# Graph and expert layer on one core: expert rows weighted on the way and added to the output by accumulating scatters, the combining stage removed

## What is computed

```
x1     = x + gnn(layernorm(x)) + attention(layernorm(x))
n      = layernorm(x1);  u = n * gamma + beta
logits = u @ Wr + br;    (top, sec), (e1, e2) = top_k(logits, 2)
w1, w2 = softmax(top, sec)
out    = x1 + w1 * expert[e1](u) + w2 * expert[e2](u)
expert[e](u) = gelu(u @ W1[e] + b1[e]) @ W2[e] + b2[e]
```

## Time and profile before

| | us |
|---|---|
| median of 3 runs | 1534.99 (1532.45 to 1539.14) |
| the profiled execution | 1534.88 |
| its span in the trace | 1532.9 |
| router block's last part, W2 load issued | 985.88 |
| first expert gather issued | 1058.74 |
| last expert scatter issued | 1461.52 |
| first load of the combining block issued | 1473.52 |

### The profile page before, as it was taken

The page is one execution under the profiler, slowest core; times in us unless marked ns, Lnnn a source line. Parts: engine busy times, 40 slices in busy tenths (PEclk is TensorE's granted clock), DMA queues, the critical chain, the costliest instruction groups (busy, mean ns, idle before and its releaser), DMA issues. The chain is left out here.

```text
span 1532.9 us, 30179 instructions
## 1 busy us (share of the span) xinstructions
PE 1266.2 (83%) x8310; PEld 1107.0 (72%) x8311; DVE 960.1 (63%) x2700; ACT 450.8 (29%) x1322; POOL 764.0 (50%) x822
## 2 busy tenths in 40 slices
PE   1797678888888999998987978767999999999910
PEld 1685477887787889887775856523999999999900
DVE  3998777777688888778854977863222223222347
ACT  1565600122123333333221023463322332233200
POOL 2001577777777777777774023201555555555400
PEclk9999898999999999999998989955999999999965
DMA  6002533333466667778895000252666666666658
GB/s 204 15 0 69 168 106 105 104 105 106 126 177 174 199 196 215 211 219 261 279 283 166 1 1 1 108 181 94 211 210 209 216 209 210 212 215 207 192 198 314
DMA packets 142678, 248.24 MB, mean 162 GB/s; under 512 B 22826, under 2 KB 99108, under 8 KB 142324
## 3 DMA queue, kind: packets, MB, share of 16 engines
q1 hardware_dynamic: 99256, 146.13, 29.8%
q0 software_dynamic: 34320, 93.76, 21.0%
q10 hardware_dynamic: 9004, 7.21, 1.4%
HBM read 213.65 MB, written 33.36 MB: 161 GB/s over the span
## 5 line engine op out<-in xcount | busy, mean ns | idle before, releaser
L716 POOL DMA_INDIRECT RG<-table,srci x504 | 496.0, 984 | 157.7 <-issue 154.4
L733 PE MATMUL ps<-S_t,RG 128*128 128x96 f32 x2016 | 283.7, 278 | 51.7 <-DMA RG<-table,srci 47.8
L733 PEld LDWEIGHTS ps<-S_t,RG 128*128 128x128 f32 x2016 | 270.3, 195 | 74.8 <-DMA RG<-table,srci 60.8
L1881 DVE TENSOR_TENSOR R<-ps,R 128x256 f32<-128x256 f32 x105 | 44.6, 425 | 278.4 <-PE ps L1833 278.4
L1823 PE MATMUL ps<-R,RG 128*128 128x128 f32 x1680 | 207.2, 277 | 0.0
L987 DVE TENSOR_TENSOR R<-R,ps 128x392 f32 x280 | 157.0, 561 | 79.3 <-PE ps L743 59.7
L755 PE MATMUL ps<-zrow,R 128*128 128x256 f32 x686 | 193.3, 386 | 12.8 <-DMA zrow<-table 7.9
L1856 ACT ACTIVATE R<-ps,RG 128x128 f32<-128x128 f32 x420 | 119.7, 368 | 279.0 <-PE ps L1823 279.0
L1833 PE MATMUL ps<-R 128*128 x840 | 198.6, 380 | 0.0
L1823 PEld LDWEIGHTS ps<-R,RG 128*128 128x128 f32 x1680 | 198.4, 194 | 0.0
L1907 POOL DMA_INDIRECT results<-R,S_t x105 | 103.7, 988 | 164.0 <-DVE R L1881 160.8
(11 more groups left out here) (352 smaller groups left out, 1883.3 us busy)
## 6 DMA issues: line engine op xcount, KB each, us to landing
RG<-in_w SPq DMA_DIRECT2D x106, 514.0 KB
zrow<-table SPq DMA_DIRECT2D x336, 128.0 KB
R<-results SPq DMA_DIRECT2D x48, 256.0 KB, 12.2
RG<-table,srci POOLq DMA_INDIRECT x504, 3.4
table<-RG SPq DMA_DIRECT2D x12, 512.0 KB, 2.9
table<-R SPq DMA_DIRECT2D x12, 512.0 KB, 3.3
out<-R ACTq DMA_DIRECT2D x48, 128.0 KB, 5.4
R<-in_x SPq DMA_DIRECT2D x6, 896.0 KB
```

The costliest lines, as they stand in the source:

```text
L716: nc.gpsimd.indirect_dma_start(out=grows[:, s, :], out_offset=None, in_=table, in_offset=bass.IndirectOffsetOnAxis(ap=srci[:, ND + q, c:c ...
L733: last = nc.tensor.matmul(window(q % 2)[:, h, :], grows[:, s, h * P:(h + 1) * P], S_t[:, q % 2, c, :], start=c == 0, stop=c == GC - 1)
```

## The change

The DRAM tensor `results` and the combining block are gone. In their place:

- SP stores x1 into the output in the router block, four tiles at a time, as `finish` produces them (`store_x1`). Twelve of the thirteen stores stand ahead of the W2 load on SP's queue.
- `table` becomes `ntable`, with rows of 258 floats: the normalised row and the row's two weights. The weights are stored with two more transfers that write runs of two floats (8 bytes), 6250 in all, between the ninth and the tenth `keep_rows`. VectorE computes the weights behind its second placing round (`row_weights`), for which ScalarE's exponential moves ahead of `norm(24)`.
- In the expert block VectorE picks the weight of the slot (`wsel`, two one-column instructions in `widen`), and behind the bias multiplies the tile by it (`weighted`). `rows` now waits for the bias alone (`b_ok`), the scatter for the product (`y_ok`).
- The scatter adds to the output (`compute_op=ALU.add`). Padding slots get a row number out of bounds, which is skipped. A row's two experts lie in different tiles, and nothing orders two additions to one row but waits, so scatter(t) waits until scatter(t-2) has landed, until `border(t)` on SP has passed (which waits for scatter(t-5), and where a new expert begins for scatter(t-1)), and for the first five tiles for scatter(t-1).
- Of VectorE's steps behind `psI`, the four that made `sct` go. Two new ones for `sct` and three for the selecting columns `first` and `second` stand at the head of VectorE's expert block, and two small ones for the borders ahead of the wait for `psI`.

```diff
-    results = nc.dram_tensor("results", (2 * N + NTILE * P, D), f32, kind="Internal").ap()
+    ntable = nc.dram_tensor("ntable", (N, D + 2), f32, kind="Internal").ap()
...
+                def store_x1(h):
+                    lo, hi = 4 * h, min(4 * h + 4, T)
+                    sp.wait_ge(x_ok, hi)
+                    if hi < T:
+                        sp.dma_start(a_out[lo * P:hi * P, :].rearrange("(t p) f -> p t f", p=P),
+                                     o_all[:, lo:hi, :]).then_inc(x1_out, 16)
+                    else:
+                        sp.dma_start(a_out[lo * P:N, :], o_all[0:TAIL, lo, :]).then_inc(x1_out, 16)
+
+                for h in range(NB4 - 1):
+                    store_x1(h)
                 sp.wait_ge(px_ok, T)
                 sp.dma_start(R3[:, 0:room], a_w2).then_inc(w2_in, 16)
-                sp.wait_ge(x_ok, T)
+                store_x1(NB4 - 1)
                 sp.dma_start(b2s.rearrange("p e f -> p (e f)"), a_b2.unsqueeze(0).to_broadcast([P, NX * D])).then_inc(b2_in, 16)
...
                     if lo + n < T:
-                        sp.dma_start(table[lo * P:(lo + n) * P, :].rearrange("(t p) f -> p t f", p=P),
+                        sp.dma_start(ntable[lo * P:(lo + n) * P, 0:D].rearrange("(t p) f -> p t f", p=P),
                                      n_rows[:, 4 * (h % NR):4 * (h % NR) + n, :]).then_inc(keep[h % NR], 16)
                     else:
-                        sp.dma_start(table[lo * P:N, :], n_rows[0:TAIL, 4 * (h % NR), :]).then_inc(keep[h % NR], 16)
+                        sp.dma_start(ntable[lo * P:N, 0:D], n_rows[0:TAIL, 4 * (h % NR), :]).then_inc(keep[h % NR], 16)
...
                 for h in range(NB4 - 4):
                     keep_rows(h)
+                sp.wait_ge(w_ok, 1)
+                sp.dma_start(ntable[0:(T - 1) * P, D:D + 2].rearrange("(t p) k -> p t k", p=P),
+                             wpair[:, 0:T - 1, :]).then_inc(w_out, 16)
+                sp.dma_start(ntable[(T - 1) * P:N, D:D + 2], wpair[0:TAIL, T - 1, :]).then_inc(w_out, 16)
                 sp.wait_ge(eid_ok, 1)
...
-                for t in range(early):
+                for t in range(24):
                     norm(t)
                 act.wait_ge(ex_in, 1)
                 act.activation(w2c[:, :], sec, ACT.Exp).then_inc(ex_ok, 1)
+                for t in range(24, early):
+                    norm(t)
                 act.wait_ge(ready, 3)
...
+                def row_weights():
+                    v.wait_ge(ex_ok, 1)
+                    ch.done(nc.vector.tensor_scalar(w1c[:, :], w2c[:, :], 1.0, None, ALU.add))
+                    ch.done(nc.vector.reciprocal(wpair[:, :, 0], w1c[:, :]))
+                    ch.done(nc.vector.tensor_tensor(wpair[:, :, 1], w2c[:, :], wpair[:, :, 0], ALU.mult))
+                    v.sem_inc(w_ok, 1)
...
+                def border_waits():
+                    turn = slot[0:1, 0, 0:NTILE]
+                    ch.done(nc.vector.tensor_tensor(turn, eidf[:, 1:NTILE + 1], eidf[:, 0:NTILE], ALU.is_gt))
+                    ch.done(nc.vector.scalar_tensor_tensor(late, turn, 16.0, late_f[:, 0:NTILE], ALU.mult, ALU.add))
+
                 for r in range(NROUND):
                     place(r)
...
+                    if r == WROUND:
+                        row_weights()
+                    if r == EROUND:
+                        expert_ids()
+                border_waits()
...
-                nc.vector.tensor_scalar(pad, held, 0.5, None, ALU.is_lt)
                 ch.done(nc.vector.tensor_scalar(held_i, held, -1.0, 0.0, ALU.add, ALU.max))
                 ch.done(nc.vector.tensor_scalar(gat, held_i, 1, None, ALU.arith_shift_right))
-                ch.done(nc.vector.tensor_tensor(pad, pad, dump, ALU.mult))
-                ch.done(nc.vector.scalar_tensor_tensor(pad, held, -1.0, pad, ALU.add, ALU.add))
-                ch.done(nc.vector.tensor_copy(sct, pad))
...
+                def border(t, s):
+
+                    n = nc.sync.value_load(late[0:1, bass.ds(t - 1, 1)], min_val=16, max_val=16 * (LOOPS + 1))
+                    sp.wait_ge(y_out[s], n)
+                    sp.sem_inc(turn_ok, 1)
+
+                for t in range(2, 9):
+                    fetch(t, t % 4)
+                with nc.sync.Fori(0, LOOPS - 2) as i:
                     for u in range(4):
-                        fetch(i * 4 + (u + 2), (u + 2) % 4)
+                        fetch(i * 4 + (u + 9), (u + 1) % 4)
+                        border(i * 4 + (u + 5), u % 4)
+                for t in range(NTILE - 4, NTILE):
+                    border(t, (t - 1) % 4)
...
-                v.sem_inc(y_ok, 2)
+                ch = Chain(v, dv)
+                ch.done(nc.vector.tensor_scalar(pad, held, 0.5, float(1 << 16), ALU.is_lt, ALU.mult))
+                ch.done(nc.vector.tensor_tensor(sct, pad, gat, ALU.add))
+                ch.done(nc.vector.tensor_scalar(held_i, held_i, 1, None, ALU.bitwise_and))
+                ch.done(nc.vector.tensor_copy(second[:, 0:NTILE], held_i))
...
                 def widen(t, s):
                     v.wait_ge(xt_ps, t + 1)
+                    nc.vector.tensor_scalar(wpart[:, s:s + 1], xr[:, s, D:D + 1], first[:, bass.ds(t, 1)], None,
+                                            ALU.mult).then_inc(wp_ok, 1)
                     for k in range(KC):
-                        last = nc.vector.tensor_scalar(ur[:, s % 2, k, :], psX[s % 2][:, k * P:(k + 1) * P],
-                                                       gamma[:, k:k + 1], beta[:, k:k + 1], ALU.mult, ALU.add)
-                    last.then_inc(u_ok, 1)
-
-                def bias(t, s, turn):
+                        nc.vector.tensor_scalar(ur[:, s % 2, k, :], psX[s % 2][:, k * P:(k + 1) * P],
+                                                gamma[:, k:k + 1], beta[:, k:k + 1], ALU.mult, ALU.add)
+                    v.wait_ge(wp_ok, t + 1)
+                    nc.vector.scalar_tensor_tensor(wsel[:, s:s + 1], xr[:, s, D + 1:D + 2], second[:, bass.ds(t, 1)],
+                                                   wpart[:, s:s + 1], ALU.mult, ALU.add).then_inc(u_ok, 1)
+
+                def weighted(t, s, turn):
                     e = nc.vector.value_load(eid_i[0:1, bass.ds(t, 1)], min_val=0, max_val=NX - 1)
                     v.wait_ge(y_ps, t + 3)
                     if not (isinstance(turn, int) and turn == 0):
                         v.wait_ge(y_out[s], turn * 16)
                     nc.vector.tensor_tensor(yr[:, s, :], psY[s % 2][:, 0:D],
                                             b2s[:, bass.ds(e, 1), :].rearrange("p a f -> p (a f)"),
-                                            ALU.add).then_inc(y_ok, 1)
+                                            ALU.add).then_inc(b_ok, 1)
+                    v.wait_ge(b_ok, t + 3)
+                    nc.vector.tensor_scalar(yr[:, s, :], yr[:, s, :], wsel[:, s:s + 1], None, ALU.mult).then_inc(y_ok, 1)
...
-                        out=xr[:, t % 4, :], out_offset=None, in_=table,
+                        out=xr[:, t % 4, :], out_offset=None, in_=ntable,
                         in_offset=bass.IndirectOffsetOnAxis(ap=gat[:, t:t + 1], axis=0)).then_inc(x_in[t % 4], 16)
 
                 def scatter(t):
-                    pool.wait_ge(y_ok, t + 3)
+                    pool.wait_ge(y_ok, t + 1)
+                    if t >= 2:
+                        pool.wait_ge(y_out[(t - 2) % 4], 16 * ((t - 2) // 4 + 1))
+                    if 1 <= t < 5:
+                        pool.wait_ge(y_out[t - 1], 16)
+                    if t >= 5:
+                        pool.wait_ge(turn_ok, t - 4)
                     nc.gpsimd.indirect_dma_start(
-                        out=results, out_offset=bass.IndirectOffsetOnAxis(ap=sct[:, t:t + 1], axis=0),
-                        in_=yr[:, t % 4, :], in_offset=None).then_inc(y_out[t % 4], 16)
+                        out=a_out, out_offset=bass.IndirectOffsetOnAxis(ap=sct[:, t:t + 1], axis=0),
+                        in_=yr[:, t % 4, :], in_offset=None, bounds_check=N - 1, oob_is_err=False,
+                        compute_op=ALU.add).then_inc(y_out[t % 4], 16)
...
-                def load(t, s, n=P):
-                    sp.dma_start(pairs[0:n, s, :], results[bass.ds(t * (2 * P), 2 * n), :]
-                                 .rearrange("(p k) f -> p (k f)", k=2)).then_inc(got[s], 16)
...
-                def combine(t, s, turn, n=P):
-                    v.wait_ge(got[s], turn * 16 + 16)
-                    x1 = o_all[0:n, bass.ds(t, 1), :].rearrange("p a f -> p (a f)")
-                    nc.vector.scalar_tensor_tensor(slotb[0:n, s % 2, :], pairs[0:n, s, 0:D], w1c[0:n, bass.ds(t, 1)],
-                                                   x1, ALU.mult, ALU.add).then_inc(mid, 1)
-                    v.wait_ge(mid, t + 1)
-                    nc.vector.scalar_tensor_tensor(pairs[0:n, s, 0:D], pairs[0:n, s, D:2 * D],
```

(50 more changed lines are left out.)

55 lines of the change are left out of this document (11 added, 44 removed).

## The result

The changed kernel takes 1524.8 us (median of 6, 1519.14 to 1526.61) against 1534.88 before: a ratio of 0.9929, 95% interval 0.9913 to 0.9945. It is faster by 0.7%, clear of noise, where 4% were forecast. Its profiled execution took 1519.14 us, the fastest of its six, with a span of 1517.2.

What follows compares the result with a forecast made beforehand. TensorE was taken to bound the expert block, ScalarE's wait for a `table` store the router block's end. Less 71.4 us of end, +4.2 for W2, -0.8 behind `psI`, plus the last scatter's needs: 1474 us; range 1468 to 1480, 8 in 10 1467 to 1495.

Steps and rivals of the forecast that it cites:

- The end: Behind the last scatter: all 71.4 us go; the new last scatter is issued at 1465.5, lands 1471.0, span 1472.4.
- W2 behind x1's stores: Router block, SP's queue: W2 and the first row store go later, ScalarE and placing matmuls too; +4.2 us (0 to 6).
- Weights, small writes: Router block: row weights and 6250 writes of 8 bytes (3.4 to 18.7 us) are covered by 35 us; cost nothing.
- Rival B: Small writes outlast the router block, with cover gone at 90 ns each; 1480 to 1500 us, chance 0.13.
- Landing of an addition: Expert block: an adding scatter lands in 4.5 us, bounds 2.7 to 6.1; its wait bites only past 7.1 us.
- Expert block, VectorE: Per tile, product, two one-column steps and waits add 1.0 to 1.4 us against 2.46 of slack; nothing in the period.
- The step that failed: Expert block: a gather delayed behind a border's waiting scatter is made good in the next tile; cost nothing.
- the treatment of POOL: Expert block: POOL idles 1.47 us ahead of each scatter, so its instruction may grow that much from 0.99; cost nothing.
- C: Expert block: the scatter's landing bites a little, or POOL's instruction grows past 2.4 us; 1480 to 1527 us, chance 0.10.
- D: Expert block: chain of scatters waiting for scatter t-2 sets the period, slower than before; landing past 8.3 us, chance 0.06.

Runs made afterwards that it cites:

- its own experiment: Changed kernel with the W2 load issued ahead of the last two stores of x1: 1522.62 us, 0.9925 of the kernel before.
- the shorter delay: Kernel before with one POOL sum of 128x320 (about 0.9 us) between each scatter and the gather behind it: ratio 1.0072.
- the one that copies: Changed kernel with the scatter copying instead of adding, all waits kept: 1488.67 us, 0.9697 of the kernel before.
- the kernel with the delay and the gather ahead: Kernel before with one POOL sum of 128x320 behind each scatter and gather t+5 put ahead of scatter t: ratio 1.0004.

## Why the prediction was wrong

- **The end: mostly right, by two errors of opposite sign.** 60.1 us fell away between last bias and end; forecast were 72.1 less about 8.2. The last scatter started at 1507.05 and landed 2.7 us later, at 1509.75, and the span ended at 1517.2. The prediction had allowed 1.0 + 4.5 us up to the landing, counting POOL's instruction twice, since a landing in these views holds it already, and 1.4 us behind it (1.9, if 1528.6 + 2.4 is the last store's landing); 7.5 us follow instead. They are nearly all one instruction of POOL's own queue at the end of the block, DRAIN; what it waits for the trace doesn't tell. It stood in the trace of before as well, inside the 12.0 us of "clearing and meeting". Its rows by line, after and then before:

```profile
L1811 POOLq DRAIN  x1: 7084/7084/7084, 1509.9 to 1509.9; - x1
```

```profile
L1775 POOLq DRAIN  x1: 8638/8638/8638, 1464.1 to 1464.1; - x1
```

  The combining block had no indirect transfer, and its DRAIN took 0.03 us at 1473.5. So removing that block moved the span's end to behind a long DRAIN.

- **W2 behind x1's stores: right in mechanism, 5.2 us instead of 4.2**, and undone by its own experiment to 0.7.
- **Weights, small writes: right.** They took 17.7 ns each in the mean, below the dearest bound of 47.9; nothing waited. Rival B did not occur. The 96 ns that the prediction estimated from the rule in the Trainium skill (DMA: Bandwidth & Descriptors, Specifications) were far too dear.
- **Landing of an addition: right in the median.** 3.9 us against 4.5, inside the bounds, with single ones up to 6.8. The median also lies in the 2.9 to 4.7 us that the prediction estimated from the Trainium skill (DMA: Bandwidth & Descriptors, Latency and other measured facts). (Its sum for them is 0.2 us low: it should read 1472.8 to 1474.6.)
- **Expert block, VectorE: right.** `widen` stayed in time.
- **The step that failed: "The gather is issued some 8 us ahead of its transpose (two periods) and lands in 3.4."** The flip of the gather issued at 1442.42, in the same timeline of the kernel before:

```profile
1447.35 0.36 PEld L1813 LDWEIGHTS ps<-ident,R 128*128 128x128 f32 x2
```

  From the bias to that flip there are 1447.35 - 1440.42 = 6.93 us, and the 2.00 us from bias to gather issue stood in the earlier trace rows and were not subtracted. The real lead was 4.9 us, for a landing of 2.8 in the median (this late one had 4.6, and still fitted). So the whole loop had 11.1 - 6.36 - 2.8 = 2.0 us to spare. The change put 1.54 us on it by POOL's queue, 1.8 in the mean, and these moved the gather up to the W1 load, which put 1.3 us on its landing. The 1.1 us over, spread over three tiles, are 0.37 us per tile, against 0.39 measured. The prediction put this term at nothing.
- **With it failed the treatment of POOL:** "may grow from 0.99 by these 1.47 us before it counts". POOL's idle time ahead of the scatter is not slack of what queues behind the scatter. POOL had time to spare in the changed kernel (it was busy for 64 of 100 us), and the shorter delay showed 0.9 us of it to cost 11 us.
- **The rivals.** C and D had the period set by the landing of scatter t-2 or by POOL's sheer load; neither came. The measured time lies in C's interval by another mechanism, which is luck. A rival "the gather becomes late behind a longer scatter" was worked out nowhere, though D named "the gather queued behind" and C a longer instruction of POOL.

## What to carry to other kernels

When an instruction on an in-order queue gets later or longer, cost it by what stands behind it: take the next instruction on that queue, the time at which its result is needed, and go round the whole loop (here three tiles) until it closes; idle time ahead of the instruction says nothing. Ask also what else goes to the DMA engines at the new time of issue: here a gather 1 to 2 us later met a load of 514 KB and landed 1.3 us later. Prefetches should be issued ahead of waiting stores as soon as their buffers are free, not in the order in which tiles are numbered. A block that is held by such a loop hides gains made elsewhere and varies between runs, so measure other edits after it is opened. When a block at the end is removed, look at what the block ahead of it does behind its last landing.

## What the runs showed of the hardware

- An indirect scatter of 128 rows of 1 KB took POOL 1.59 us with an addition and 1.01 without. Its landing, counted from the instruction's start, was 3.9 us against 2.5. With the addition it went out in packets of 1024 bytes instead of 4096, and POOL's queue took 39.3% of the DMA engines' time for 6.41 MB against 21.7% for 7.08 MB.
- An indirect gather of 128 rows landed in 2.8 us in the median when a load of 514 KB was issued 1.0 to 2.4 us behind it, and in 4.1 (plain scatters) to 4.6 us (adding ones) when that load was issued less than 0.7 us behind it or just ahead: so in the kernel before, the changed one and the one that copies. With the gather further ahead and additions the first figure was 3.3 to 3.9 us.
- POOL's DRAIN at the end of the expert block started 0.2 us behind the last landing and took 7.0 or 7.1 us with adding scatters and 8.6 with plain ones in every kernel here; in the combining block, without indirect transfers, 0.03 us.
- The time from a wait's release to an indirect scatter's start grew from 0.27 to 0.83 us with the changed scatter's three waits and its bounds check, added or not; which of them does it was not separated.
- Writes of 8 bytes into DRAM took 17.7 ns of one DMA engine each in the mean, 7.7 to 49 by stretches of 1 or 2 us.
- On one of the chips the unchanged kernel took 1673.5 us instead of 1535; the expert block of the kernel with the delay and the gather ahead ran there at 3.714 us per tile too, so what differed lay elsewhere.
